# A top-p threshold search with fewer passes and a wider sorted window

## The reference

```python
def _adj_from_feats(Xa, W1, W2, W3):
    logits = (Xa @ W1) @ W2 @ (Xa @ W3).T          # 2048 x 2048
    order = jnp.argsort(-logits, axis=1)
    vals  = jnp.take_along_axis(logits, order, axis=1)
    csum  = jnp.cumsum(jax.nn.softmax(vals, axis=1), axis=1)
    k_i   = jnp.sum(csum < 0.9, axis=1) + 1         # per row: how many to keep
    ... # the k_i largest stay, the others become -inf
    return jax.nn.softmax(masked, axis=1)
for s in range(2):                                  # R: row-normalised x1 matrix, fixed
    A = _adj_from_feats(Xa, W1, W2, W3)
    Xf, Xa = R @ Xf, A @ Xa
    Z = Z + (Xf @ U1s[s] + Xa @ U2s[s])
return layernorm(X + Z) * gamma + beta
```

## Time and profile before

| | |
|---|---|
| time, median of 3 runs | 1350.34 us (1349.93 to 1350.79) |
| span of the profiled execution, first to last instruction | 1347.3 us |
| PE busy | 1193.1 us (89%) |
| DVE busy | 1089.4 us (81%) |
| ACT, POOL busy | 573.3, 259.7 us |
| granted TensorE clock, mean | 0.96 |

### The profile page before, as it was taken

The page is one execution under the profiler, slowest core; times in us unless marked ns, Lnnn a source line. Parts: engine busy times, 40 slices in busy tenths (PEclk is TensorE's granted clock), DMA queues, the critical chain, the costliest instruction groups (busy, mean ns, idle before and its releaser), DMA issues.

```text
span 1347.3 us, 17786 instructions
## 1 busy us (share of the span) xinstructions
PE 1193.1 (89%) x6042; PEld 587.6 (44%) x6042; DVE 1089.4 (81%) x1865; ACT 573.3 (43%) x1092; POOL 259.7 (19%) x236
## 2 busy tenths in 40 slices
PE   0578999999898997999995999898999999799893
PEld 0233555554343454554553554243454454354451
DVE  7887777753999899999899004999999899899778
ACT  2634454537422455554543437560462563231130
POOL 6032232321323011021021001321101111012011
PEclk9888999999999899999997999999999999899897
DMA  7136565632344000001000004236313313313364
GB/s 233 57 108 216 194 231 178 225 139 70 113 126 155 2 32 32 2 32 44 37 32 33 16 16 141 86 106 232 101 48 102 102 48 101 103 32 100 92 231 172
DMA packets 55774, 138.76 MB, mean 103 GB/s; under 512 B 9536, under 2 KB 9536, under 8 KB 51584
## 3 DMA queue, kind: packets, MB, share of 16 engines
q1 hardware_dynamic: 55680, 137.66, 30.6%
HBM read 88.10 MB, written 49.55 MB: 102 GB/s over the span
## 4 chain that ended last, share of the span: by engine, by line
DVE 58%; PE 23%; issue 9%; ACT 3%; DMA 3%; DVEq 1%; SPq 1%; POOL 0%; POOLq 0%; ACTq 0%
DVE WS L1499 20%; DVE w L1722 5%; PE UB L720 4%; DVE g L1582 4%; DVE E L1685 4%; DVE WS L1720 3%; PE AB L710 3%; PE AB L703 3%; DVE WS L1719 3%; PE RB L720 3%; PE XB L720 2%; PE AB L901 1%; DMA E<-adjT 1%; PE RB L901 1%; DMA Khl<-z_d 1%
## 5 line engine op out<-in xcount | busy, mean ns | idle before, releaser
L1499 DVE SCALAR_TENSOR_TENSOR WS<-E,g 128x2048 bf16<-128x2048 f32 x128 | 311.8, 2486 | 1.2
L1582 DVE TENSOR_REDUCE g<-E 128x1 f32<-128x2048 f32 x32 | 73.0, 2281 | 106.9 <-ACT E L1143 106.3
L1221 ACT ACTIVATE turns<-TB 128x512 f16<-128x512 f32 x128 | 75.6, 594 | 138.8 <-PE TB L735 138.8
L729 PE MATMUL TB<-ident,E 128*128 128x128 f32 x512 | 81.9, 289 | 40.0 <-DVEq L1787 38.8
L607 POOL TENSOR_TENSOR RT<-RT,AD 128x512 f32<-128x512 f32 x32 | 53.0, 1657 | 286.4 <-ACT RT L1197 285.3
L1685 DVE SCALAR_TENSOR_TENSOR E<-E,g 128x2048 f32<-128x2048 f32 x34 | 82.9, 2469 | 17.9 <-issue 17.2
L729 PEld LDWEIGHTS TB<-ident,E 128*128 128x128 f32 x512 | 66.8, 149 | 65.0 <-DVEq L1787 31.3
L1215 ACT ACTIVATE turns<-TB 128x512 f16<-128x512 f32 x128 | 75.6, 594 | 37.2 <-PE TB L729 37.1
L1143 ACT ACTIVATE E<-LB 128x512 f32<-128x512 f32 x128 | 75.7, 599 | 13.0 <-PE LB L810 11.7
L624 POOL TENSOR_TENSOR XHL<-WF,XHL 128x512 f16<-128x512 f32 x16 | 23.5, 1466 | 286.6 <-ACT XHL L1236 286.6
L1722 DVE MAX8 w<-WS 128x8 f32<-128x2048 f32 x32 | 73.4, 2295 | 1.1
(11 more groups left out here) (314 smaller groups left out, 2361.0 us busy)
## 6 DMA issues: line engine op xcount, KB each, us to landing
turns<-adj_parts SPq DMA_DIRECT2D x48, 512.0 KB, 3.8
E<-adjT SPq DMA_DIRECT2D x16, 1024.0 KB, 7.6
adj_parts<-turns SPq DMA_DIRECT2D x16, 1024.0 KB, 5.2
AH<-adj_parts SPq DMA_DIRECT2D x16, 512.0 KB, 4.0
z_d<-UO SPq DMA_DIRECT2D x31, 256.0 KB, 2.3
XR<-x SPq DMA_DIRECT2D x4, 1024.0 KB, 11.9
WS<-U SPq DMA_DIRECT2D x4, 1024.0 KB, 7.7
x_d<-E SPq DMA_DIRECT2D x16, 256.0 KB, 2.0
```

Source lines behind the costliest of these rows:

```text
L729: i = mm(bank[:, k * P:(k + 1) * P], src(k), ident32[:, :], is_transpose=True, start=(k == 0), stop=(k == KC - 1), skip_group_check=True)
L1221: a(ET[:, 1, c * KC:(c + 1) * KC, :].rearrange("p b c -> p (b c)"), TB[c % 2][:, :], ACT.Copy, scale=SE).then_inc(s_et, 1)
L1499: return v.scalar_tensor_tensor(junk[t % 2], e, g4[:, k, t:t + 1], e, op, ALU.mult, accum_out=g4[:, F_, t:t + 1])
L1582: ct(v.tensor_reduce(row(A2)[:, t:t + 1], E[:, slot, :], AX.X, ALU.max))
```

## The change

`search` makes one pass with `s_of` in step 0 and two in step 1 (`SEARCH - 1`). The point is moved by `by_width` after the first and by `by_slope` after the second, and aimed above the threshold, by 14 or 9 weights of the point's size. Then a last instruction per tile, over 2048 columns, writes the weights below the point to `WS` and sums them; `max` gives the eight largest of each of 16 parts of 128 columns. `settle` sorts the 32 largest of these 128 candidates by four rounds of `max` and three of `match_replace`, all on 128 columns, forms the running sum with one scan over 4x33 values, and reads the threshold off. A row is flagged for `bisect` if the mass above the point is already 90%, if the 32nd is at or above the threshold, if a part gave eight at or above it, or with eight or more equal weights to drop; for `in_order` with one or more. What follows (the flags' way to the register, masks, repairs, `largest`) is as before. The core of the diff:

```diff
-SEARCH = (4, 4)
+SEARCH = (2, 3)
+AIM = ((14.0,), (9.0, 14.0))
+PARTS = 16
+PART = N // PARTS
+WIDE = 32
...
+            def few_left(ct):
+                ct.free(v.scalar_tensor_tensor(row(CAPU), row(U), FEW, row(TGT), ALU.mult, ALU.is_ge))
+            def capped(ct):
+                ...            # 3 instructions on 128x4
+            def by_width(ct, aim, last):
+                ...            # 8 waited for and 4 free on 128x4, and capped/few_left if last
+            def by_slope(ct, aim):
+                ...            # 14 waited for and 8 or 9 free on 128x4, and capped
...
             def search(g, gq, ct):
...
-                for it in range(SEARCH_N):
+                for it in range(SEARCH_N - 1):
                     for slot, t in tiles:
...
                         ct(s_of(E[:, slot, :], t, U, ALU.is_ge), behind=(1 if t < G - 1 else 0))
...
+                for slot, t in tiles:
+                    ct(v.scalar_tensor_tensor(WS[:, :], E[:, slot, :], g4[:, U, t:t + 1], E[:, slot, :], ALU.is_lt,
+                                              ALU.mult, accum_out=g4[:, F_, t:t + 1]))
+                    for c in range(PARTS):
+                        i = v.max(cand[:, t, 8 * c:8 * c + 8], WS[:, c * PART:(c + 1) * PART])
+                    ct(i)
...
             def settle(g, gq, ct):
...
-                for slot, t in tiles:
-                    ct(v.tensor_scalar(WS[:, :], E[:, slot, :], g4[:, HI, t:t + 1], None, ALU.subtract))
-                    ct(v.tensor_scalar(bits(WS[:, :]), bits(WS[:, :]), bits(g4[:, FLIP, t:t + 1]), None,
-                                       ALU.bitwise_xor))
-                    ct(v.max(w8[:, t, :], WS[:, :]))
-                ...            # some 25 small instructions
+                ct.free(v.tensor_tensor(win[:, :, 0], row(DLO), row(F_), ALU.subtract))
+                ct.free(v.tensor_reduce(row(FULL), cand[:, :, 7:8 * PARTS:8], AX.X, ALU.max))
+                for k in range(WIDE // 8):
+                    for t in range(G):
+                        ct(v.max(win[:, t, 1 + 8 * k:9 + 8 * k], cand[:, t, :]), behind=G - 1)
+                    if k < WIDE // 8 - 1:
+                        for t in range(G):
+                            ct(v.match_replace(cand[:, t, :], win[:, t, 1 + 8 * k:9 + 8 * k], cand[:, t, :], 0.0),
+                               behind=G - 1)
+                ct(v.tensor_tensor_scan(*flat, 0.0, ALU.mult, ALU.add))
+                ct(v.tensor_scalar(ge[:, :, :], run[:, :, :], 0.0, None, ALU.is_ge))
+                ...            # 7 waited for and 5 free small ones: THR, FULL, BAD, flags
```

More of the change, by code:

```diff
@@ L1366, in _ @@
                 v.tensor_scalar(rstd[:, tiles], mv[:, tiles, 1], EPS, None, ALU.add).then_inc(s_lnvar, 1)
[L1367 to L1368 removed]
+            ch(v.memset(gate[:, :, :], 1.0))
+            ch.free(v.memset(gate[:, :, 0], 0.0))
             ch(v.memset(flag[:, :], 0.0))
@@ new lines, in by_width @@
+            def by_width(ct, aim, last):
+                per_sig = TOP_P / (2 * PHI_P)
+                ct(v.tensor_tensor(row(D_), row(F_), row(TGT), ALU.subtract))
+                ct.free(v.tensor_copy(g4[:, UP:DP + 1, :], g4[:, U:D_ + 1, :]))
+                if last:
+                    few_left(ct)
+                ct(v.scalar_tensor_tensor(row(A1), row(U), aim, row(D_), ALU.mult, ALU.add))
+                ct.free(v.scalar_tensor_tensor(row(X_), row(A1), per_sig, row(RS), ALU.mult, ALU.mult))
+                ct(v.scalar_tensor_tensor(row(LOW), row(A1), 0.0, row(A2), ALU.min, ALU.mult))
+                ct.free(v.tensor_scalar(row(LOW), row(LOW), -BELOW_BEND * TOP_P, 1.0, ALU.mult, ALU.add))
+                ct(v.tensor_scalar(row(A1), row(X_), -BEND, LEAST - 1.0, ALU.mult, ALU.max))
+                ct(v.tensor_tensor(row(A1), row(A1), row(LOW), ALU.add))
+                ct(v.reciprocal(row(A1), row(A1)))
+                ct(v.tensor_tensor(row(A1), row(A1), row(X_), ALU.mult))
+                ct(v.scalar_tensor_tensor(row(U), row(A1), 1.0, row(U), ALU.add, ALU.mult))
+                if last:
+                    capped(ct)
+                else:
+                    ct(v.tensor_scalar(row(U), row(U), E_TOP, None, ALU.min))
@@ L1649, in search @@
                         ct(s_of(E[:, slot, :], t, U, ALU.is_ge), behind=(1 if t < G - 1 else 0))
[L1650 to L1655, removed]
@@ L1656, in search @@
-                    if it == 0:
[L1658 to L1681, removed]
@@ new lines, in search @@
+                    if it == 0:
+                        by_width(ct, AIM[s][0], SEARCH_N == 2)
+                    else:
+                        by_slope(ct, AIM[s][1])
+                for slot, t in tiles:
[4 more added lines that the diff above has]
+                    ct(i)
@@ L1702, in settle @@
                 tiles, sl = slots_of(g)
[L1703 to L1715, removed]
@@ L1723, in settle @@
[L1723 to L1728, removed]
@@ L1730, in settle @@
[L1730 to L1741, removed]
@@ L1750, in settle @@
-                ct(v.tensor_tensor(row(A1), row(A1), h8[:, :, WIN - 1], ALU.max))
-                ct(v.scalar_tensor_tensor(row(A1), row(BAD), 1.5, row(A1), ALU.is_gt, ALU.mult))
-                ct(v.scalar_tensor_tensor(flag[:, 1:5], ge[:, :, WIN - 1], 0.0, row(A1), ALU.is_equal, ALU.max))
-                ct(v.scalar_tensor_tensor(flag[:, 5:9], row(BAD), 1.5, flag[:, 1:5], ALU.is_gt, ALU.max))
+                wide = [P, G, WIDE]
+                below = win[:, :, 1:]
+                ct.free(v.tensor_tensor(win[:, :, 0], row(DLO), row(F_), ALU.subtract))
@@ new lines, in settle @@
+                dve.wait_ge(c_dve, ct.base + ct.n)
+                flat = (u[:, :, :].rearrange("p g k -> p (g k)") for u in (run, gate, win))
+                ct(v.tensor_tensor_scan(*flat, 0.0, ALU.mult, ALU.add))
+                ct(v.tensor_scalar(ge[:, :, :], run[:, :, :], 0.0, None, ALU.is_ge))
+                ct(v.tensor_tensor(run[:, :, 1:], ge[:, :, 1:], below, ALU.mult))
+                ct.free(v.tensor_tensor(row(FULL), row(FULL), win[:, :, WIDE], ALU.max))
+                ct(v.tensor_reduce(row(THR), run[:, :, 1:], AX.X, ALU.max))
@@ new lines, in settle @@
+                ct.free(v.tensor_tensor(run[:, :, 1:], below, row(THR).unsqueeze(2).broadcast_to(wide), ALU.is_equal))
+                ct(v.tensor_tensor(row(FULL), row(FULL), row(THR), ALU.is_ge))
+                ct(v.tensor_tensor(run[:, :, 1:], run[:, :, 1:], ge[:, :, 0:WIDE], ALU.mult))
+                ct.free(v.tensor_tensor(row(FULL), row(FULL), ge[:, :, 0], ALU.max))
+                ct(v.tensor_reduce(row(BAD), run[:, :, 1:], AX.X, ALU.add))
+                ct(v.scalar_tensor_tensor(flag[:, 1:5], row(BAD), WIN - 0.5, row(FULL), ALU.is_gt, ALU.max))
@@ L1754, in settle @@
+                ct(v.scalar_tensor_tensor(flag[:, 5:9], row(BAD), 0.5, flag[:, 1:5], ALU.is_gt, ALU.max))
+                ct.free(v.tensor_scalar(row(BAD), row(BAD), 1.0, None, ALU.add))
                 ct.free(v.scalar_tensor_tensor(row(SAFE), flag[:, 5:9], 0.0, row(THR), ALU.is_equal, ALU.mult))
```

66 lines of the change are left out of this document (39 added, 27 removed).

## The result

The changed kernel takes 1485.15 us (median of 4 runs, 1484.61 to 1485.88), the kernel before 1350.13 us beside it (4 runs): ratio 1.1003 [1.0979, 1.1027]. The forecast was 1298.5 us, the range 1287 to 1316. What happened is rival (d), to which the prediction gave 12%.

A forecast was written before the change was run, and what follows sets the result against it. The prediction took PE to bound the groups, held up by five waits for DVE: 38.8 + 9 (clock) - 3 (stalls) + 7 (tail) = 51.8 us off a span of 1347.3, plus 3.0 around it, 1298.5 us; range 1287 to 1316.

The forecast's parts named there:

- rival (d): Search window misses a row, so its tile goes through `bisect`: slower, 1403 to 1450 us; chance 12%.
- All five waits go: PE's five waits for DVE's semaphore behind a group's first two masks vanish, 38.8 us.
- (a): Rival: DVE is the bound and its whole saving, 164 us, is the gain, 1186 us; chance 2%.
- (b): Rival: DVE's small instructions cost more than the upper prices, so PE waits in step 1, 1326 us; chance 5%.
- DVE's cost: `search` and `settle` per group, from priced small instructions: 47.6 us instead of 75.0 in step 0, 60.9 in step 1.
- Slack at the masks: DVE has a group's first masks ready before PE needs them, by 32 us in step 0 and 24 in step 1.
- The clock: PE no longer runs at a lower clock behind the first four waits: 9 us gained, 2.2 each.
- A granted clock of 1.00 behind every start: Sign of being right: PE runs at full granted clock behind the start of every group.
- The stalls for ACT: PE's stalls for ACT at group starts grow a little where PE no longer comes late: 3 us lost.
- The tail: From PE's last start to DVE's end: output loads come earlier with `s_kept`, so GpSimd starts sooner, 7 us gained.
- 3.0 us around the span: Median time less profiled span, added to the predicted span of 1295.5 us to give 1298.5.
- rival (c): Tail gives nothing because the output chain meets another load: 1305 us, within the forecast's range and its 79%.

The follow-up runs named there:

- `e1_aim145`: The changed kernel with the second aim of step 1 at 14.5 weights instead of 14: 1312.96 us, ratio 0.973, no `bisect`.
- `e4_third_pass`: The changed kernel with a third search pass in step 1 (SEARCH = (2, 4)), aims unchanged: 1325.52 us, ratio 0.9816, no `bisect`.
- `e7_exps_first`: `e1_aim145` with ACT's first two exponentials of groups 2 and 3 of step 0 moved into the last tile of the group two before: 1306.34 us, ratio 0.9669.
- `e6_loads_first`: `e1_aim145` with SP's first output loads issued behind the first R tile of the last group instead of the fourth: 1326.25 us, ratio 0.9805.
- `e8_all`: The changed kernel with a third pass in step 1, window behind `largest`, plus the reorderings of `e6_loads_first` and `e7_exps_first`: 1344.87 us, ratio 0.9964.
- `e9_best`: `e7_exps_first` with SP's first output loads issued behind the third R tile of the last group: 1306.2 us, ratio 0.9679.
- `e11_z_first`: `e9_best` with the z rows of tiles 14 and 15 loaded ahead of those tiles' own output stores in SP's queue: 1307.3 us, ratio 0.9683.
- `e10_best_third`: `e9_best` with a third pass in step 1, the window behind `largest`, and aims back at 9 and 14: 1309.91 us, ratio 0.9708.

## Why the prediction was wrong

**The step that failed** is the judgement in rival (d) that the window hits in every row: it got 88 of 100 without support. The prediction said itself that the profile can't tell, and then took the two repairs for equal weights as a sign that flags wouldn't change. They come from the data; whether a flag for `bisect` comes depends on the last point, and this step was new: four bracketing passes had given way to one or two estimates. 4096 rows have to hit, and the worst decides. One row short by less than one weight turned 37 us gained (`e1_aim145`) into 135 us lost. The range, which had left (d) outside, couldn't hold the time.

**The price of (d)** was 165 us for `bisect` and 15 for `rank_equals`, 180 us less the slack. Measured are 172.8 and 21.8, and 7.8 for the repair for equal weights, which the price left out: it runs three times in the changed kernel and twice in `e1_aim145`, where the first tile of this group needs none. So the repair was 22 us too small. The slack in that group was 45 us: without the repair the first mask would have ended at 992.4 + 2.3, and PE came at 1039.9; 202.4 - 45.2 = 157.2 us are left, the wait. (d)'s interval of 1403 to 1450 us fell short of 1485, though this slack was larger than the 28 us behind its upper end. It started from 1298.5 us where, as below, the kernel without a repair takes 1313, and it had no term for what PE loses around a long stop: against `e1_aim145` its busy time is 9.3 us longer (1192.6 for 1183.3) and its stalls for ACT 9.5 us longer (22.6 for 13.1). 157.5 + 9.3 + 9.5 = 176.3; the spans differ by 174.7.

**What holds without the repair** is seen in `e1_aim145`, term by term:

- All five waits go: right, 38.8 us. DVE isn't the bound; (a) and (b) are out.
- DVE's cost: a `max` comes every 3.19 / 16 = 0.20 us (forecast 0.22), a `match_replace` with its value load comes every 0.26 us (forecast 0.22), the scan takes 0.43 (forecast 0.3); a group 49.7 us for 47.6. DVE's busy time is 912.2 us, forecast 925.
- Slack at the masks: in group 1 of step 0, from the end of the second mask at 490.15 to PE's start at 524.58, 34.4 us (forecast 32); ahead of the last group, 1203.94 to 1232.80, 29 us (forecast 24). Right, but it isn't the only place where DVE's time counts: `e4_third_pass` showed ACT waiting for `largest` with no such slack.
- The clock: for the same instructions PE's busy time falls by 9.8 us, 7.4 of them up to its last start (1138.1 to 1130.7), where 9 were forecast. A granted clock of 1.00 behind every start, named as a sign, didn't come: behind the first two starts it was 0.79 (436 to 441 us) and 0.73 (527 to 534 us), where PE waits for ACT.
- The stalls for ACT: L738's line goes from 4.2 us (L735 before) to 13.1, 8.9 us for the 3 forecast. I had read 1.01 us at one start without a wait and taken it for all; at the others the wait for DVE had hidden ACT's lateness. `e7_exps_first` gets 4.6 us of it back.
- The tail: 7 us forecast, 1.9 came. The loads were issued 2.5 us earlier behind PE's last start, GpSimd's first addition began 2.7 us earlier (19.9 for 22.6), and the chain behind it took 0.7 us longer. I took the loads to follow `s_kept`; they follow SP's queue, in which the R tiles' stores come first. `e6_loads_first` and `e8_all` show the queue at work, `e9_best` and `e11_z_first` that the last blocks take back what the first gains: rival (c).

The sum as measured: 38.8 + 7.4 - 8.9 + 1.9 = 39.2 us, and the spans differ by 38.0; small waits elsewhere take the 1.2 us. Against the forecast's 51.8 us the stalls lack 5.9, the tail 5.1, the clock 1.6 and the small waits 1.2: these 13.8 us are why the version without a repair has a span of 1309.3 us and not of 1295.5. Rival (c) held, but it is only the tail's part; the stalls cost more than it. The prediction also put 3.0 us around the span; every run of the record has 1.9 (1485.88 us for a span of 1484.0).

The best versions of these, `e7_exps_first` and `e9_best`, take 1306.3 and 1306.2 us: 44 us less than before, 179 less than the change as it stood. Their aim is fitted to these inputs with hardly a weight to spare: by the same calculation the thresholds of step 1 lie 2nd to 31st of the 32 in the window, and an aim of 15 would flag another row, too deep. `e10_best_third` keeps them at 2nd to 27th, for 3.7 us.

## What to carry to other kernels

Where a faster path is guarded by a repair that costs 200 us, the chance of the repair is the forecast: work out on the inputs how close the worst row comes to the guard before pricing the path, and when nothing can be worked out, let the range reach to the repair. When a wait goes, read every other start with the wait's cover taken away, since the next late engine is hidden under it. A load that is to come earlier comes no earlier than what stands before it in its queue, and a semaphore wait that is moved ahead there holds up all that follows.

## What the runs showed of the hardware

- Sixteen independent `max` over 128 columns take 3.19 us, 0.20 each, while the mean of one is 277 ns: they overlap by 0.08 us. The Trainium skill ("VectorE: DVE Perf Modes", the DRAIN section) says that the next instruction starts when the pipe is empty, but also that one which is not held back starts earlier. The prediction took only the first from it; the trace agrees with the second.
- A `match_replace` over 128 columns is two instructions, 78 and 274 ns. The second takes no longer than a `max` (277), so it doesn't take twice the time for its data; together they come every 0.26 us. The scan over 132 values takes 433 ns, half as much again as a `max`.
- In the 157.5 us for which PE stood, its granted clock went down to the lower level (0.50 from 1060 to 1160 us), and the 7 us behind it ran at 0.54:

```profile
1197.00:1204.00 7.00, 6.32 (x21) 3.58 (x22) 6.97 (x7) 4.49 (x6) 0.00 (x0) 0.54 0.00 0
```
